# Local attention of a tuned transformer stack: V as weights, turned probabilities moving, denominators by products with ones

## The chip, the core and the metric

The kernel runs on one core of one Trainium2 chip. The metric is the device time of one execution in microseconds (us); lower is better. TensorE multiplies matrices into PSUM, VectorE and ScalarE read PSUM and do the elementwise work, GpSimd helps on SBUF, SyncE issues transfers. All arrays of this case fit in SBUF, and the program is written out by hand: each engine has its own list of instructions, and semaphores order them against each other.

## What is computed

A chain of four layers on x of shape (8, 128, 128): a cross attention with relative positions, a quantised feed-forward layer, a second cross attention, and the stage that this document is about, a local-attention transformer of depth 2. It takes the 8 blocks of x one by one, 128 tokens each; the window is 64.

```python
DIM, DEPTH, HEADS, DIM_HEAD, WINDOW = 128, 2, 8, 64, 64

def local_attention(q, k, v):            # q, k, v: (b, 8 heads, n, 64)
    ...                                  # windows of 64 look at themselves and at the one before
    sim = jnp.einsum('bhwid,bhwjd->bhwij', bq, bk)
    sim = jnp.where(mask, -jnp.finfo(sim.dtype).max, sim)
    attn = jax.nn.softmax(sim, axis=-1)
    out = jnp.einsum('bhwij,bhwjd->bhwid', attn, bv)
    ...

def _layer(x, wqkv, qs, ksc, wo, lg, lb, w1, b1, w2, b2):
    h = shift_token(x)
    q, k, v = jnp.split(h @ wqkv, 3, axis=-1)          # then split into heads
    q, k = rotary_xpos(l2norm(q) * qs, l2norm(k) * ksc)
    o = local_attention(q, k, v)
    x = x + o.transpose(0, 2, 1, 3).reshape(b, n, 512) @ wo
    ...                                  # shift, layer norm, w1, a * gelu(g), w2, residual
```

## The kernel before

The stages run one after another; the first three take about the first 320 us and are not touched. In the local stage a *tile* is one block n of 128 tokens in layer l, with all 8 heads; there are 8 tiles in each of 2 layers. Everything is float32, and a float32 product shows as two pairs of weight load and matmul in the trace, a turn (a transpose through TensorE) as one. A tile goes through these steps; the names are those of the functions.

- `qkv` (TensorE): three products of 512 columns into banks 0 to 2. ScalarE squares q and k (`square`) and copies V to `VL` (`take_v`).
- `rotate` (VectorE): rotary tables and sums of squares; `head_root` (ScalarE) and `unit_norm` (VectorE) finish the norm of the heads.
- `turn_qk` (TensorE, 8 turns into banks 5 and 6), `take_turned_qk` (ScalarE, two copies).
- `score` (TensorE): the band mask and 8 heads of 64 rows, even and odd heads in the two halves of the rows, into banks 3 and 4. `largest` (VectorE) takes the row maximum, `shift` (TensorE) subtracts it, `exponential` (ScalarE) writes the probabilities, tokens on the partitions.
- `turn_p` (TensorE, 8 turns into banks 5 and 6), `take_turned_p` (ScalarE, two copies to `P1`: keys on the partitions).
- `weigh` (TensorE, L547): for each head the turned probabilities are the weights and V of that head moves, with a 65th column of ones, so that the same product gives the denominator. The output has tokens on the partitions.
- `divide_output` (VectorE): a reciprocal of the 8 denominators of each token (L1002) and a multiply into `LO` (L1006).
- `turn_o` (TensorE, L521, 4 turns of the output into bank 7), `take_turned_o` (ScalarE, L1215, one copy to `LOT`), `project_o` (TensorE, L527, 4 products with `wo`), `add_output` (VectorE, L996).

TensorE's order in the loop over tiles n sets how the steps interleave: `shift(n)`, `qkv(n+2)`, `turn_qk(n+1)`, `turn_o(n-1)`, `turn_p(n)`, `project_o(n-1)`, `score(n+1)`, `weigh(n)`. VectorE's is `largest(n)`, `divide_output(n-1)`, `unit_norm(n+1)`, `rotate(n+2)`, `add_output(n-1)`. ScalarE's is `exponential(n)`, `square(n+2)`, `take_turned_qk(n+1)`, `take_turned_o(n-1)`, `take_v(n+2)`, `take_turned_p(n)`, `head_root(n+2)`. In tiles 6 and 7 parts of the feed-forward layer come in between (`turn_norm`, `hidden`, `gate`), and after tile 7 follow `hidden(2)`, `turn_o(7)`, `project_o(7)` and `down(0)`, while ScalarE loads an activation table between its last `take_gelu` and `take_turned_o(7)`.

Of the kernel before, what the change touches and what calls it, by code (L numbers as in the profile page):

```python
# [17 lines left out]
ALU = mybir.AluOpType  # L18
ACT = mybir.ActivationFunctionType
AX = mybir.AxisListType  # L20

P = 128
# [62 lines left out]
def build(nc, x_d, ctxT_d, maskT_d, const_d, l0_d, ffn0_d, l1_d, f_d, out_d):  # L85
    with ExitStack() as stack:
# [108 lines left out]
        VL = view(blkf, 9216, 3, LH, LD + 1)  # L195
        LO = view(blkf, 10776, 2, 512)
        LOT = full[:, 0, 0:512].rearrange("p (a b) -> p a b", a=4)
# [30 lines left out]
        def _(pe):  # L228
# [285 lines left out]
            def turn_o(l, n):  # L514
                pe.wait_ge(sem("lo_norm"), NB * l + n + 1)
                if n >= 1:
                    pe.wait_ge(sem("z"), NB + 10 * l + n)
                else:
                    pe.wait_ge(sem("zT"), 2 * l + 2)
                for j in range(4):  # L520
                    i = tr(ps[:, 7, P * j:P * (j + 1)], LO[:, n % 2, P * j:P * (j + 1)], ident)  # L521
                i.then_inc(sem("loT_ps"), 1)

            def project_o(l, n):
                pe.wait_ge(sem("loT"), NB * l + n + 1)
                for j in range(4):
                    i = mm(ps[:, 7, 0:P], LOT[:, j, :], w_f[:, l, F_WO + P * j:F_WO + P * (j + 1)], start=(j == 0), stop=(j == 3))  # L527
                i.then_inc(sem("lwo_ps"), 1)
# [11 lines left out]
            def weigh(l, n):  # L540
                b = NB * l
                pe.wait_ge(sem("qkv_read"), b + n + 1)
                for h in range(LH):
                    if h % 4 == 0:
                        pe.wait_ge(sem("p_turned"), 2 * (b + n) + h // 4 + 1)
                    s = 2 * (h % 4) + h // 4
                    i = mm(ps[:, 5 + h // 4, 65 * (h % 4):65 * (h % 4 + 1)], P1[:, n % 2, P * h:P * (h + 1)],  # L547
                           VL[:, n % 3, s, :], start=(h % 4 == 0), stop=True, skip_group_check=True)
                i.then_inc(sem("lo_ps"), 1)
# [54 lines left out]
            for l in range(2):  # L604
                for n in range(NB):
# [7 lines left out]
                    if n >= 1:  # L613
                        turn_o(l, n - 1)
                    turn_p(l, n)
                    if n >= 1:
                        project_o(l, n - 1)
# [10 lines left out]
                turn_o(l, NB - 1)  # L628
# [20 lines left out]
        def _(dve):  # L649
# [348 lines left out]
            def divide_output(l, n):  # L998
                b = NB * l
                dve.wait_ge(sem("lo_ps"), b + n + 1)  # L1000
                o = ps[:, 5:7, 0:260].rearrange("p b (h d) -> p b h d", h=4)
                step(v.reciprocal(lrec[:, :].rearrange("p (b h) -> p b h", b=2), o[:, :, :, LD]))  # L1002
                settle()
                if n >= 2:
                    dve.wait_ge(sem("loT_ps"), b + n - 1)
                v.tensor_tensor(LO[:, n % 2, :].rearrange("p (h b d) -> p b h d", b=2, h=4), o[:, :, :, 0:LD],  # L1006
                                lrec[:, :].rearrange("p (b h o) -> p b h o", b=2, h=4).to_broadcast([P, 2, 4, LD]),
                                ALU.mult).then_inc(sem("lo_norm"), 1)
# [60 lines left out]
        def _(act):  # L1069
# [140 lines left out]
            def take_turned_o(l, n):  # L1210
                b = NB * l
                act.wait_ge(sem("loT_ps"), b + n + 1)
                if b + n >= 1:
                    act.wait_ge(sem("lwo_ps"), b + n)
                a(LOT, ps[:, 7, :].rearrange("p (j t) -> p j t", j=4), ACT.Copy).then_inc(sem("loT"), 1)  # L1215

# [53 lines left out]
            for l in range(2):  # L1270
                for n in range(NB):
# [12 lines left out]
                    if n >= 1:  # L1284
                        take_turned_o(l, n - 1)
# [10 lines left out]
                take_turned_o(l, NB - 1)  # L1296
# [22 lines left out]
        def _(pool):  # L1319
# [27 lines left out]
            g_.memset(VL[:, :, :, LD:LD + 1], 1.0).then_inc(sem("pool_zeroed"), 1)  # L1347
            pool.wait_ge(sem("blocks"), 4)
            pool.wait_ge(sem("pool_zeroed"), 1)
# [48 lines left out]
```

## Time and profile before

| | us |
|---|---|
| median of 3 runs (lowest to highest) | 597.12 (596.97 to 600.94) |
| the profiled execution | 598.13 |
| its span | 596.2 |
| TensorE matmul busy in the span | 460.5 (77%) |
| VectorE busy | 416.3 (70%) |
| ScalarE busy | 217.5 (36%) |
| mean granted clock of TensorE | 0.868 of 2.4 GHz |

Engines in the rows: PE is TensorE's matmul, PEld its weight load, DVE is VectorE, ACT is ScalarE, POOL is GpSimd. L527 is line 527 of the kernel. A row in order of time reads: start, length, engine, line, operation, out<-in, shapes, count, and in brackets how long the engine had been idle and what ended that. Rows of the same kind that follow each other are merged into one, so its length spans them all. Matmuls are pipelined: each shows some 0.2 to 0.3 us of its own length while they start 0.05 to 0.2 us apart. The granted clock (PEclk) is 1.00 at 2.4 GHz and 0.50 at 1.2 GHz.

### The profile page before, as it was taken

Reading aid. Unit: us, or ns where it says so; the run is one execution under the profiler, and the core shown is the slowest. Engines: PE = TensorE matmul, PEld = TensorE weight load, DVE = VectorE, ACT = ScalarE, POOL = GpSimd, SP = SyncE. Lnnn points to the kernel's source line nnn. Section 1 sums busy time; section 2 is a strip of 40 time slices with the busy share of each in tenths; the row PEclk is TensorE's granted clock in tenths of the full one; section 3 lists DMA queues with packets and bytes.
Section 4 is the critical chain, followed back from the end, with each engine's and each line's share of the span. In section 5 each row is a group of like instructions: output and inputs, shape, how many; then the busy total and the mean of one; then the engine's idle time right before and its main releaser. Section 6 shows DMA issues by size and latency. Waiting matters only on the chain.

```text
span 596.2 us, 10352 instructions
## 1 busy us (share of the span) xinstructions
PE 460.5 (77%) x4308; PEld 350.0 (59%) x4309; DVE 416.3 (70%) x834; ACT 217.5 (36%) x365; POOL 28.2 (5%) x21
## 2 busy tenths in 40 slices
PE   4379999989824377889886568989787588987946
PEld 2268999979611235767784136667563456766733
DVE  6989977892287888988624638788526668878331
ACT  2324333331233123334432234454534445454431
POOL 3400000000000040000000000000000000001010
PEclk9879999997655577878976869999989899997998
DMA  8200000001000000000000000000000000000000
GB/s 346 106 2 2 3 4 3 3 2 36 1 1 0 0 1 1 1 0 2 1 0 2 0 0 1 1 1 1 1 1 0 0 1 2 1 1 1 1 18 18
DMA packets 1630, 8.43 MB, mean 14 GB/s; under 512 B 177, under 2 KB 177, under 8 KB 1329
## 3 DMA queue, kind: packets, MB, share of 16 engines
q1 hardware_dynamic: 1584, 7.78, 3.4%
q8 instruction: 34, 0.56, 0.4%
q14 instruction: 12, 0.09, 0.0%
HBM read 7.26 MB, written 0.52 MB: 13 GB/s over the span
## 4 chain that ended last, share of the span: by engine, by line
PE 54%; DVE 31%; ACT 8%; issue 6%; DMA 1%; ACTq 0%; DVEq 0%
PE ps L232 15%; PE ps L477 8%; PE ps L329 5%; PE ps L547 4%; PE ps L583 3%; PE ps L449 3%; DVE blk L730 3%; PE ps L527 3%; PE ps L537 2%; DVE m L923 2%; DVE PT L927 2%; PE ps L307 2%; DVE blk L744 2%; PE ps L592 2%; PE ps L244 1%
## 5 line engine op out<-in xcount | busy, mean ns | idle before, releaser
L477 PE MATMUL ps<-w_f,full 128*128 128x512 f32 x96 | 49.3, 654 | 5.4 <-DVE blk L969 3.7
L232 PE MATMUL ps<-blk,stA 128*128 128x64 bf16 (+1 forms) x576 | 47.5, 223 | 3.5 <-issue 3.5
L1128 ACT ACTIVATE St<-ps 128x512 f32<-128x512 f32 x32 | 19.2, 599 | 73.3 <-PE ps L232 73.3
L965 DVE TENSOR_TENSOR blk<-ps,tabs 128x1024 f32<-128x1024 f32 x16 | 19.6, 1224 | 35.5 <-ACT blk L1198 35.5
L232 PEld LDWEIGHTS ps<-blk,stA 128*128 128x128 bf16 x576 | 33.6, 102 | 13.4 <-issue 6.8
L329 PE MATMUL ps<-V,PT 128*64 128x9 f32 x512 | 38.5, 214 | 0.0
L329 PEld LDWEIGHTS ps<-V,PT 128*64 128x64 f32 x512 | 36.3, 155 | 2.5
L449 PEld LDWEIGHTS ps<-V,PT 128*128 128x128 f32 x256 | 37.7, 234 | 0.0
L232 PE MATMUL ps<-blk,stB 128*128 128x64 bf16 (+1 forms) x288 | 37.7, 222 | 0.0
L1173 ACT ACTIVATE PT<-PT 128x1024 f32<-128x1024 f32 x16 | 16.9, 1057 | 56.8 <-DVE PT L927 56.8
L449 PE MATMUL ps<-V,PT 128*128 128x9 f32 x256 | 37.1, 283 | 0.0
L477 PEld LDWEIGHTS ps<-w_f,full 128*128 128x128 f32 x96 | 20.0, 212 | 27.8 <-issue 24.6
L547 PE MATMUL ps<-blk,PT 128*128 128x65 f32 x256 | 31.6, 276 | 0.0
L547 PEld LDWEIGHTS ps<-blk,PT 128*128 128x128 f32 x256 | 30.0, 192 | 2.4 <-issue 1.0
L841 DVE TENSOR_REDUCE mneg<-ps 128x4 bf16<-128x512 f32 x32 | 21.9, 687 | 12.9 <-PE ps L307 12.8
L730 DVE TENSOR_TENSOR blk<-blk,const 128x512 bf16<-128x512 bf16 x48 | 30.1, 682 | 0.0
L730 DVE TENSOR_TENSOR blk<-part,const 128x512 bf16<-128x512 bf16 x48 | 30.0, 682 | 0.0
L436 PE MATMUL ps<-const,PT 128*128 128x128 f32 x128 | 20.3, 311 | 12.5 <-ACT PT L1180 10.9
L232 PEld LDWEIGHTS ps<-blk,stB 128*128 128x128 bf16 x288 | 26.6, 100 | 5.3 <-issue 2.7
L923 DVE TENSOR_REDUCE m<-ps 128x8 f32<-128x1024 f32 x16 | 19.5, 1221 | 13.3 <-PE ps L232 13.3
L436 PEld LDWEIGHTS ps<-const,PT 128*128 128x128 f32 x128 | 17.2, 162 | 18.6 <-ACT PT L1173 16.3
L537 PE MATMUL ps<-const,PT 128*128 128x128 f32 x128 | 17.8, 285 | 12.6 <-ACT blk L1223 12.6
(200 smaller groups left out, 1021.7 us busy)
## 6 DMA issues: line engine op xcount, KB each, us to landing
w_f<-f_dram SPq DMA_DIRECT2D x2, 1689.0 KB, 13.7
w_x<-l_dram SPq DMA_DIRECT2D x1, 774.0 KB, 6.6
w_f<-ffn_dram SPq DMA_DIRECT2D x1, 561.0 KB, 8.3
w_f<-l_dram SPq DMA_DIRECT2D x1, 514.0 KB, 3.6
X<-x_dram SPq DMA_DIRECT2D x1, 512.0 KB, 3.6
ctxT<-ctxT_dram SPq DMA_DIRECT2D x1, 512.0 KB, 4.8
OT<-maskT_dram SPq DMA_DIRECT2D x1, 512.0 KB, 7.4
out_dram<-Z SPq DMA_DIRECT2D x2, 256.0 KB, 2.0
```

The source lines that it names most:

```text
L232: return mm(out, l, r, start=start, stop=False, skip_group_check=True)
L329: i = mm(o[:, n % 4, h, :], pt[:, h, n, q:q + 64], V[:, n, HG * g + h, :], start=(n % 4 == 0 and h == 0), stop=True, skip_group_check=True)
L436: i = tr(ps[:, 4 + c, P * j:P * (j + 1)], S1[:, u % 2, P * (4 * c + j):P * (4 * c + j + 1)], ident)
L449: i = mm(o[:, n % 4, h, :], P1[:, u % 2, P * h:P * (h + 1)], V[:, n, HG * g + h, :], start=(n % 4 == 0 and h == 0), stop=True, skip_group_ ...
L477: i = mm(ps[:, c, :], hT[:, n, :], W[:, F_QKV + 512 * c:F_QKV + 512 * (c + 1)], start=True, stop=True)
L537: i = tr(ps[:, 5 + c, P * j:P * (j + 1)], S1[:, n % 2, P * (4 * c + j):P * (4 * c + j + 1)], ident)
L547: i = mm(ps[:, 5 + h // 4, 65 * (h % 4):65 * (h % 4 + 1)], P1[:, n % 2, P * h:P * (h + 1)], VL[:, n % 3, s, :], start=(h % 4 == 0), stop=T ...
L730: i = v.tensor_tensor(ring[:, c % RING, b, :, :, :], src.to_broadcast([P, NB, QC, HG]), keep.to_broadcast([P, NB, QC, HG]), ALU.mult)
L841: v.tensor_reduce(mneg[:, c % 2, :], ps[:, 4 + c % 2, :].rearrange("p (j k) -> p j k", j=4), AX.X, ALU.max).then_inc(sem("chunk_max"), 1)
L923: step(v.tensor_reduce(m1[:, u % 2, :], s, AX.X, ALU.max))
L965: step(v.tensor_tensor(heads(R[:, n % 2, :]), u, tab[:, 0].to_broadcast([P, 2, LH, LD]), ALU.mult))
L1128: a(St[:, i % 2, :], ps[:, i % 4, :], ACT.Copy).then_inc(sem("st_copied"), 1)
```

## The change

`weigh` swaps its operands. V of a head becomes the weights (64 columns) and the turned probabilities move (128 columns), so the output has the head's 64 features on half of the partitions and the tokens along the free axis: it is already turned. Even heads write partitions 0 to 63, odd heads 64 to 127, of bank 5. The denominators come from 8 more products with a matrix of ones as weights, into bank 6, where each of 64 partitions holds the same sums. `divide_output` takes the reciprocal of all of bank 6 (128 x 512) into the new buffer `over`, and multiplies bank 5 by it straight into `LOT`, which becomes double. `turn_o` and `take_turned_o` go; `project_o` stands where `turn_o` stood. `VL` loses its column of ones. `weigh` waits for both halves of `P1` at its start.

```diff
--- before.py
+++ after.py
@@ -192,9 +192,9 @@
         T2 = view(blkf, 5120, T)
         QT = view(blkf, 6144, 2, 4, P)
         KT = view(blkf, 7168, 2, 4, P)
-        VL = view(blkf, 9216, 3, LH, LD + 1)
-        LO = view(blkf, 10776, 2, 512)
-        LOT = full[:, 0, 0:512].rearrange("p (a b) -> p a b", a=4)
+        VL = view(blkf, 9216, 3, LH, LD)
+        over = view(blkf, 10776, 512)
+        LOT = full[:, 0, :].rearrange("p (s a b) -> p s a b", s=2, a=4)
         hT = full[:, 1, :].rearrange("p (n t) -> p n t", n=NB)
 
         ps = stack.enter_context(nc.psum_tensor("ps", [P, 8, 512], F32))
@@ -511,20 +511,15 @@
                             lneg[:, n % 2, 4 * c:4 * c + 4].rearrange("p (h o) -> p h o", o=1).to_broadcast([P, 4, P]))
                 i.then_inc(sem("lshifted"), 1)
 
-            def turn_o(l, n):
+            def project_o(l, n):
                 pe.wait_ge(sem("lo_norm"), NB * l + n + 1)
                 if n >= 1:
                     pe.wait_ge(sem("z"), NB + 10 * l + n)
                 else:
                     pe.wait_ge(sem("zT"), 2 * l + 2)
                 for j in range(4):
-                    i = tr(ps[:, 7, P * j:P * (j + 1)], LO[:, n % 2, P * j:P * (j + 1)], ident)
-                i.then_inc(sem("loT_ps"), 1)
-
-            def project_o(l, n):
-                pe.wait_ge(sem("loT"), NB * l + n + 1)
-                for j in range(4):
-                    i = mm(ps[:, 7, 0:P], LOT[:, j, :], w_f[:, l, F_WO + P * j:F_WO + P * (j + 1)], start=(j == 0), stop=(j == 3))
+                    i = mm(ps[:, 7, 0:P], LOT[:, n % 2, j, :], w_f[:, l, F_WO + P * j:F_WO + P * (j + 1)],
+                           start=(j == 0), stop=(j == 3))
                 i.then_inc(sem("lwo_ps"), 1)
 
             def turn_p(l, n):
@@ -540,12 +535,17 @@
             def weigh(l, n):
                 b = NB * l
                 pe.wait_ge(sem("qkv_read"), b + n + 1)
+                pe.wait_ge(sem("p_turned"), 2 * (b + n) + 2)
                 for h in range(LH):
-                    if h % 4 == 0:
-                        pe.wait_ge(sem("p_turned"), 2 * (b + n) + h // 4 + 1)
-                    s = 2 * (h % 4) + h // 4
-                    i = mm(ps[:, 5 + h // 4, 65 * (h % 4):65 * (h % 4 + 1)], P1[:, n % 2, P * h:P * (h + 1)],
-                           VL[:, n % 3, s, :], start=(h % 4 == 0), stop=True, skip_group_check=True)
+                    d, j = LD * (h % 2), h // 2
+                    mm(ps[d:d + LD, 5, P * j:P * (j + 1)], VL[:, n % 3, h, :],
+                       P1[:, n % 2, P * (4 * (h % 2) + j):P * (4 * (h % 2) + j + 1)],
+                       start=(j == 0), stop=True, skip_group_check=True)
+                for h in range(LH):
+                    d, j = LD * (h % 2), h // 2
+                    i = mm(ps[d:d + LD, 6, P * j:P * (j + 1)], ones[:, 0:LD],
+                           P1[:, n % 2, P * (4 * (h % 2) + j):P * (4 * (h % 2) + j + 1)],
+                           start=(j == 0), stop=True, skip_group_check=True)
                 i.then_inc(sem("lo_ps"), 1)
 
 
@@ -611,10 +611,8 @@
                     if n + 1 < NB:
                         turn_qk(l, n + 1)
                     if n >= 1:
-                        turn_o(l, n - 1)
+                        project_o(l, n - 1)
                     turn_p(l, n)
-                    if n >= 1:
-                        project_o(l, n - 1)
                     if n + 1 < NB:
                         score(l, n + 1)
                     if n == 6:
@@ -625,7 +623,6 @@
                     if n == 5:
                         shift_tokens(l, 0)
                 hidden(l, 2)
-                turn_o(l, NB - 1)
                 project_o(l, NB - 1)
                 down(l, 0)
                 shift_tokens(l, 1)
@@ -998,14 +995,12 @@
             def divide_output(l, n):
                 b = NB * l
                 dve.wait_ge(sem("lo_ps"), b + n + 1)
-                o = ps[:, 5:7, 0:260].rearrange("p b (h d) -> p b h d", h=4)
-                step(v.reciprocal(lrec[:, :].rearrange("p (b h) -> p b h", b=2), o[:, :, :, LD]))
-                settle()
-                if n >= 2:
-                    dve.wait_ge(sem("loT_ps"), b + n - 1)
-                v.tensor_tensor(LO[:, n % 2, :].rearrange("p (h b d) -> p b h d", b=2, h=4), o[:, :, :, 0:LD],
-                                lrec[:, :].rearrange("p (b h o) -> p b h o", b=2, h=4).to_broadcast([P, 2, 4, LD]),
-                                ALU.mult).then_inc(sem("lo_norm"), 1)
+                step(v.reciprocal(over, ps[:, 6, :]))
+                settle()
+                if b + n >= 2:
+                    dve.wait_ge(sem("lwo_ps"), b + n - 1)
+                v.tensor_tensor(LOT[:, n % 2, :, :].rearrange("p a b -> p (a b)"), ps[:, 5, :], over, ALU.mult)\
+                    .then_inc(sem("lo_norm"), 1)
 
             unit_banks = ((0, 1), (3, 4), (0, 1), (3, 4), (5, 6), (3, 4))
 
@@ -1207,13 +1202,6 @@
                 act.wait_ge(sem("ss"), NB * l + n + 1)
                 root(ss[:, :], lss[:, :], lr0[:, :], "root")
 
-            def take_turned_o(l, n):
-                b = NB * l
-                act.wait_ge(sem("loT_ps"), b + n + 1)
-                if b + n >= 1:
-                    act.wait_ge(sem("lwo_ps"), b + n)
-                a(LOT, ps[:, 7, :].rearrange("p (j t) -> p j t", j=4), ACT.Copy).then_inc(sem("loT"), 1)
-
             def take_turned_qk(l, n):
                 b = NB * l
                 act.wait_ge(sem("qkT_ps"), b + n + 1)
@@ -1281,8 +1269,6 @@
                         take_turned_qk(l, n + 1)
                     if n == 6:
                         norm_root(4 + 2 * l)
-                    if n >= 1:
-                        take_turned_o(l, n - 1)
                     if n + 2 < NB:
                         take_v(l, n + 2)
                     take_turned_p(l, n)
@@ -1293,7 +1279,6 @@
                 take_gelu(l, 1)
                 take_gelu(l, 2)
                 nc.scalar.preload_act_table_set(roots)
-                take_turned_o(l, NB - 1)
                 take_halves(l, 1)
                 if l == 0:
                     take_turned_z(1, 0)
@@ -1344,9 +1329,8 @@
             add_bias(1, w_x1, 3 * NB)
 
             pool.wait_ge(sem("scores1"), G * NB)
-            g_.memset(VL[:, :, :, LD:LD + 1], 1.0).then_inc(sem("pool_zeroed"), 1)
             pool.wait_ge(sem("blocks"), 4)
-            pool.wait_ge(sem("pool_zeroed"), 1)
+            pool.wait_ge(sem("bias_added"), 2)
             g_.memset(hT[64:128, :, 0:1], 0.0).then_inc(sem("local_zeroed"), 1)
             bias_row = lambda t: t.rearrange("p (o e) -> p o e", o=1).to_broadcast([P, 4, P])
             for l in range(2):
```

TensorE's list in a full tile of layer 0, from the shift on. The names are the functions above: L232 with `lneg` is `shift`, L477 `qkv`, L491 `turn_qk`, L521 `turn_o`, L537 `turn_p`, L527 `project_o`, L232 with `band_b` and `blk` `score`, L547 `weigh`. Before:

```order
L232 MATMUL ps<-lneg,ident_b 128x512 x2
L477 MATMUL ps<-w_f,full 128x512 x3
L491 MATMUL ps<-const,blk 128x128 x8
L521 MATMUL ps<-const,blk 128x128 x4
L537 MATMUL ps<-const,PT 128x128 x8
L527 MATMUL ps<-w_f,full 128x128 x4
L232 MATMUL ps<-band_b,ident_b 128x512 x2
L232 MATMUL ps<-blk 128x128 x8
L547 MATMUL ps<-blk,PT 128x65 x8
```

The same tile in the changed kernel, where L521 is `project_o`, L532 `turn_p`, L541 and L546 the two halves of `weigh`:

```order
L232 MATMUL ps<-lneg,ident_b 128x512 x2
L477 MATMUL ps<-w_f,full 128x512 x3
L491 MATMUL ps<-const,blk 128x128 x8
L521 MATMUL ps<-w_f,full 128x128 x4
L532 MATMUL ps<-const,PT 128x128 x8
L232 MATMUL ps<-band_b,ident_b 128x512 x2
L232 MATMUL ps<-blk 128x128 x8
L541 MATMUL ps<-PT,blk 64x128 x8
L546 MATMUL ps<-PT,ones 64x128 x8
```

The four turns are gone, the projection stands ahead of `turn_p`, and `weigh` has 16 products instead of 8.

VectorE's list in the same place, from the row maximum to the first step of `rotate`. Before:

```order
L991 TENSOR_REDUCE lneg<-ps 128x8
L1002 RECIPROCAL lrec<-ps 128x8
L1006 TENSOR_TENSOR blk<-ps,lrec 128x2x4x64
L680 TENSOR_TENSOR lnt<-lr 128x16
L682 SCALAR_TENSOR_TENSOR lnt<-lnt,ss 128x16
L684 SCALAR_TENSOR_TENSOR lr<-lnt,lr 128x16
L983 TENSOR_TENSOR blk<-blk,lr 128x1024
L965 TENSOR_TENSOR blk<-ps,tabs 128x1024
```

In the changed kernel (`over` lies in the buffer `blk`, `LOT` in `full`):

```order
L988 TENSOR_REDUCE lneg<-ps 128x8
L998 RECIPROCAL blk<-ps 128x512
L1002 TENSOR_TENSOR full<-ps,blk 128x512
L677 TENSOR_TENSOR lnt<-lr 128x16
L679 SCALAR_TENSOR_TENSOR lnt<-lnt,ss 128x16
L681 SCALAR_TENSOR_TENSOR lr<-lnt,lr 128x16
L980 TENSOR_TENSOR blk<-blk,lr 128x1024
L962 TENSOR_TENSOR blk<-ps,tabs 128x1024
```

The order of the list is the same; the reciprocal has grown from 8 to 512 elements in each partition.

TensorE's list at a layer's end, from the last unit of the hidden layer's first half (L583, weights 85 wide) to `down` (L592). Before:

```order
L583 MATMUL ps<-YT,w_f 85x512 x2
L521 MATMUL ps<-const,blk 128x128 x4
L527 MATMUL ps<-w_f,full 128x128 x4
L592 MATMUL ps<-w_f,PT 128x128 x12
L559 MATMUL ps<-Z,const 128x256
```

And in the changed kernel:

```order
L583 MATMUL ps<-YT,w_f 85x512 x2
L521 MATMUL ps<-w_f,full 128x128 x4
L592 MATMUL ps<-w_f,PT 128x128 x12
L559 MATMUL ps<-Z,const 128x256
```

Here the turns go and the projection follows the hidden unit at once.

## Rows read from the trace of the kernel before

**Rows 1.** The page, part 4: the chain that ended last, share of the span by engine
```profile
PE 54%; DVE 31%; ACT 8%; issue 6%; DMA 1%; ACTq 0%; DVEq 0%
```

**Rows 2.** Order of time, one full tile of layer 0: start us, us, engine, line, op [idle before]
```profile
405.35 0.61 PE L232 MATMUL ps<-lneg,ident_b 128*128 128x512 bf16 x2
405.41 0.21 DVE L1002 RECIPROCAL lrec<-ps 128x8 f32<-128x8 f32 x1
...
405.65 0.69 DVE L1006 TENSOR_TENSOR blk<-ps,lrec 128x512 f32<-128x512 f32 x1
405.79 2.74 PE L477 MATMUL ps<-w_f,full 128*128 128x512 f32 x6
...
406.26 0.16 DVE L680 TENSOR_TENSOR lnt<-lr 128x16 f32<-128x16 f32 x1
...
406.88 1.22 DVE L983 TENSOR_TENSOR blk<-blk,lr 128x1024 f32<-128x1024 f32 x1
...
408.37 1.04 PE L491 MATMUL ps<-const,blk 128*128 128x128 f32 x8
408.57 1.03 ACT L1198 ACTIVATE blk<-ps 128x1024 f32<-128x1024 f32 x1 [1.55 <-PE ps L477]
...
409.24 0.60 PE L521 MATMUL ps<-const,blk 128*128 128x128 f32 x4
...
409.63 1.22 DVE L965 TENSOR_TENSOR blk<-ps,tabs 128x1024 f32<-128x1024 f32 x1 [1.52 <-ACT blk L1198]
...
410.71 1.06 PE L537 MATMUL ps<-const,PT 128*128 128x128 f32 x8 [0.87 <-ACT blk L1223]
...
411.61 1.06 PE L527 MATMUL ps<-w_f,full 128*128 128x128 f32 x8
...
412.51 0.59 PE L232 MATMUL ps<-band_b,ident_b 128*128 128x512 bf16 x2
...
413.03 1.16 PE L232 MATMUL ps<-blk 64*128 64x128 f32 x16
...
414.12 2.00 PE L547 MATMUL ps<-blk,PT 128*128 128x65 f32 x16
...
414.82 1.21 DVE L991 TENSOR_REDUCE lneg<-ps 128x8 bf16<-128x1024 f32 x1
...
416.16 0.21 DVE L1002 RECIPROCAL lrec<-ps 128x8 f32<-128x8 f32 x1
```

**Rows 3.** VectorE's groups by form, whole span: xcount | busy us, mean ns | idle before
```profile
L1002 DVE RECIPROCAL lrec<-ps 128x8 f32<-128x8 f32 x16 | 3.3, 206 | 3.9 <-PE ps L547 2.7
...
L767 DVE RECIPROCAL rec<-ps 128x32 f32<-128x32 f32 x8 | 2.8, 352 | 22.6 <-PE ps L329 13.0 <-PE ps L449 9.5
...
L808 DVE RECIPROCAL winv<-wsc 128x1 f32<-128x1 f32 x5 | 0.8, 163 | 0.2
```

**Rows 4.** Order of time, the first attention stage, 64-wide weights, 16 instructions
```profile
99.34 1.10 PE L329 MATMUL ps<-V,PT 128*64 128x9 f32 x16
```

**Rows 5.** Order of time, tiles 6 and 7 of layer 0: reciprocals and a hidden unit
```profile
428.18 0.21 DVE L1002 RECIPROCAL lrec<-ps 128x8 f32<-128x8 f32 x1 [1.09 <-PE ps L547]
...
428.41 1.88 PE L583 MATMUL ps<-YT,w_f 128*128 128x512 f32 x4
...
436.82 0.21 DVE L1002 RECIPROCAL lrec<-ps 128x8 f32<-128x8 f32 x1 [0.26 <-PE ps L547]
```

**Rows 6.** Order of time, end of layer 0: the last output projection
```profile
441.20 1.16 PE L527 MATMUL ps<-w_f,full 128*128 128x128 f32 x8 [2.25 <-ACT full L1215]
```

**Rows 7.** Order of time, TensorE after its two longest holes in the tiles
```profile
419.98 1.09 PE L491 MATMUL ps<-const,blk 128*128 128x128 f32 x8 [2.94 <-DVE blk L983]
...
546.45 1.97 PE L491 MATMUL ps<-const,blk 128*128 128x128 f32 x8 [3.71 <-DVE blk L983]
```

**Rows 8.** Stretches of 10 us: us, busy of each engine, PEclk, DMA share, GB/s
```profile
415.00:425.00 10.00, 6.23 (x51) 4.95 (x51) 7.89 (x24) 4.86 (x11) 1.26 (x1) 1.00 0.01 2
...
545.00:555.00 10.00, 8.14 (x55) 7.21 (x56) 5.47 (x19) 3.34 (x8) 0.31 (x1) 0.67 0.00 0
```

## The prediction

> **What bounds the kernel now.** I read four views, in this order: the page, the order of time through one tile of the local attention, the groups of VectorE by form, and the last tiles of a layer. The page says that TensorE holds 54% of the chain that ended last and VectorE 31% [rows 1], an average over stages. The change touches only the last 240 us of the span, the sixteen tiles (two layers of eight) of local attention, so I read one tile there [rows 2].
>
> A tile takes 10.75 us (reciprocal at 405.41 to reciprocal at 416.16) [rows 2], and most of the sixteen look like it. Two loops run through it, nearly equal. TensorE: the shift at 405.35, three projections, turning q and k (408.37), turning the output (409.24), a wait of 0.87 us for ScalarE's copies of q and k, turning the probabilities (410.71), the output projection (411.61), the next scores (412.51 and 413.03) and `weigh` (414.12 to 416.12) [rows 2]. VectorE: it idles 1.52 us for ScalarE's square, begins `rotate` at 409.63 and works on without a gap to the end of the row maximum, 414.82 + 1.21 = 416.03. From the shift to there is 10.68 us: the next shift waits for that maximum. So faster matmuls alone save almost nothing in a full tile, since the maximum still ends at 10.68.
>
> A third loop is not critical today: the reciprocal (405.41), the multiply (405.65), Newton step (406.26), head norm (406.88 to 408.10), then turning q and k (408.37) [rows 2]. TensorE is busy with the projections until then (405.79 + 2.74 = 408.53), so VectorE's path hides behind them with next to no slack. This is the path on which the change puts work.
>
> **Part by part, in one full tile.**
>
> *Removed.* Four turns of the output, 409.24 to the next free slot (0.47 us of TensorE), and one copy by ScalarE. The turns fill a hole: after them TensorE waits 0.87 us anyway [rows 2]. The projection (8 instructions, 411.61 to 412.51, 0.90 us) moves into their place, into the same hole, ahead of `turn_p`. So the stretch from `turn_p` to the reciprocal loses 0.90 us.
>
> *Weigh.* Before: 16 instructions (8 products, two passes each), 2.00 us, 0.12 us apart [rows 2]. After: 32 instructions, V or ones as 64-wide weights, 128 columns moving, heads alternating between the halves of the output. The trace has no such instruction. Two neighbours bound it. The scores alternate between the two halves of the rows with 128 columns moving: 16 instructions in 1.16 us, of which about 0.29 is one's own length, so (1.16 - 0.29)/15 = 0.058 us apart [rows 2]. Instructions with 64-wide weights and 9 columns, in one half: (1.10 - 0.20)/15 = 0.060 [rows 4], so the weight loads can keep that pace. Full-width products with 128 columns: (1.06 - 0.27)/7 = 0.113 [rows 2]. If the column halves overlap as the row halves do, `weigh` takes 31 x 0.058 + 0.25 = 2.05 us; if not, 31 x 0.11 + 0.25 = 3.65 us. I take 2.05 because the scores are nearest in pattern, and keep 3.65.
>
> *Reciprocal.* Before, 8 elements per partition; after, 512. This decides the case. The trace has reciprocals of 1, 8 and 32 elements at 163, 206 and 352 ns [rows 3]. From 8 to 32 they rise by 146/24 = 6.1 ns an element, against about 1 ns for ordinary VectorE work: 1220 ns for 1024 elements, 690 for 512 [rows 2]. Extended, 206 + 504 x 6.1 = 3.28 us, against 0.21. The lower bound is that long reciprocals stream like the multiply, 0.69 us; the rise could then come from the strided read that both of these have, which the new one hasn't. I take 3.28: two sizes on one line that also passes near 163 at one element speak for a cost of each element.
>
> *The new loop.* Put the reciprocal's start at 0. The multiply starts at 3.3, the Newton step 0.61 later (406.26 - 405.65), the head norm 0.62 after it, ending 1.22 later: 5.75. Turning q and k, 0.27 behind (408.10 to 408.37): 6.02. To `turn_p`, which includes ScalarE's copies, 2.34 (410.71 - 408.37): 8.36; the projection fits in front. To the scores 0.90: 9.26. Scores 1.61 (412.51 to 414.12): 10.87. `weigh` 2.05, to the next reciprocal: 12.92 us. Each duration not named otherwise is from [rows 2]. Do the others fit under it? VectorE works 5.75 + 5.19 (409.63 to 414.82) + 1.21 = 12.15 us of it, so it still has 0.8 us over. The new period is 12.92 against 10.75: +2.17. TensorE's wait before turning q and k grows from nothing to 6.02 - 3.2 = 2.8 us (the projections still end 3.2 after the shift).
>
> *Per layer.* Reciprocals 1 to 5: five periods. I give the first 0.2 less, since the tile that opens a layer is not yet in the rhythm: 1.95 + 4 x 2.17 = +10.6. Tile 6 took 12.02 (416.16 to 428.18); the same sum plus 0.45 for four turns of the norm (4 x 0.113) gives 13.4, or 14.5 if VectorE is held up by about 1.1 there as it was before; +1.9 in the middle. Tile 7 took 8.64 (428.18 to 436.82) [rows 5]: now the projection waits for the multiply, 4.0 us after the reciprocal's start, then 0.9 + 0.9 for `turn_p`, 1.72 for one unit of the hidden layer [rows 5] and 2.05 for `weigh`: 9.6, +0.9. At the layer's end the projection began 441.20 - 436.82 = 4.38 us after the reciprocal, held by an activation-table load and the copy on ScalarE [rows 5, 6]. Now nothing but the multiply holds it, 3.3 + 0.69 + 0.05 = 4.04: -0.3. The gain that the removed copy could bring here is eaten by the reciprocal. A layer: 10.6 + 1.9 + 0.9 - 0.3 = +13.1; both, +26.2.
>
> *The clock.* A tile now has a 2.8 us hole on TensorE. In this trace it idled 2.94 us before 419.98 and stayed at 2.4 GHz (granted 1.00), and idled 3.71 before 546.45 and fell to 1.2 GHz, granted 0.67 over that stretch [rows 7, 8]. There the same eight turns took 1.97 us for 1.09, about 0.9 more [rows 7]. The new hole lies just below the harmless one, but there are a dozen. `turn_p`, scores or `weigh` at half speed cost 1 to 2 us each time. I put in four such falls, +6; none to ten is possible, 0 to +18.
>
> *The sum.* The profiled execution took 598.1 us (span 596.2), the median of the runs is 597.1; I add to the median. 597.1 + 26.2 + 6 = 629 us. The memset of the ones column that goes, and the new wait of GpSimd in its place, lie far from any bound: nothing.
>
> **Rivals.**
> - *A, the forecast, 0.50:* reciprocal about 3.3 us, halves overlap. 629, itself 618 to 643.
> - *B, the column halves run one after the other, 0.27:* `weigh` 3.65, period 14.5, +1.6 in the 14 tiles where `weigh` lies in the loop, +22: 651. For it: nothing in the trace shows column halves side by side. Against it: row halves do it. The Trainium skill is of two minds: "TensorEngine Tiling (Array Packing)", Key Properties, lets different tiles load and multiply in parallel; "TensorE: Matmul & The Clock Gate", Part 3, The mechanism, says that a weight load overlaps running matmuls only when its row group differs, which speaks against this change.
> - *C, a long reciprocal streams, 0.10:* 0.69 us. The third loop falls to 12.92 - 2.59 = 10.3, below the 10.7 of the row maximum, so full tiles stand still. The ends gain: in tile 7 the projection no longer waits for ScalarE (-1.2), and at the layer's end down-projection can start some 2.2 earlier. -3.4 a layer: 590, faster by 1.1%. It decides once the reciprocal takes under 3.3 - 2.1 = 1.2 us. Against it: 352 ns for 32 elements.
> - *D, a longer step for each element, 0.13:* eight of VectorE's steps of 1.04 ns (1220 - 690 ns over 512 elements [rows 2]) are 8.3 ns, 4.4 us for 512, +1.1 in 14 tiles and a longer hole, some +17: 646. Against it: 6.1 measured. The Trainium skill, "VectorE: DVE Perf Modes", the 8-slice walkthrough, "First, the fixed hardware budget", says that the reciprocal repeats its divide steps eight times; the rise in [rows 3] agrees in kind and is a little smaller.
>
> **The numbers.** Slower by over 1% (about what a measurement here can tell from no change): A, B and D, 0.90, less the chance that clock and gaps favour it: 0.89. Faster by over 1%: the better part of C, 0.06. Within 1%: 0.05. The range leaves out C (0.10) and B with D together or A with many falls of the clock: 612 to 662.
>
> **What would show it.** The reciprocal's row: 16 instructions of 128x512, 3.3 us each. Reciprocals 12.9 us apart in full tiles. A wait of turning q and k for the head norm, near 2.8 us. `weigh` with its 32 instructions 0.058 apart (A) or 0.11 (B). No wait for the copy at the layer's end. Wrong would be a reciprocal under 1.2 us, or a period of 12.1 or less, which would mean that VectorE alone bounds the tile.

## The result and the profile after

| | before | changed |
|---|---|---|
| median, us | 599.03 | 632.43 |
| runs, us | 596.97 to 608.08 (4) | 630.03 to 636.68 (4) |
| span of the profiled execution, us | 596.2 | 628.3 |
| mean granted clock | 0.868 | 0.845 |

The changed kernel is slower by 5.8%: ratio 1.0577, 95% interval 1.0479 to 1.0676. The forecast was 629 us. The execution of 608.08 us fell in a slower state of the chip and is left out of the ratio, though not of the median.

The page of the changed kernel, the shares of the chain that ended last and the costliest group:

```profile
PE 49%; DVE 41%; ACT 4%; issue 4%; DMA 1%; DVEq 0%; ACTq 0%
...
L998 DVE RECIPROCAL blk<-ps 128x512 f32<-128x512 f32 x16 | 53.7, 3356 | 10.1 <-PE ps L546 10.1
```

VectorE's share of the chain rose from 31% [rows 1] to 41%, and the reciprocal is the costliest group of the kernel: 16 instructions of 3.36 us, 53.7 us, where the old one took 0.21 us each [rows 3].

One full tile of layer 0 in order of time, the same stretch of work as in [rows 2] (start, length, engine, line, operation, idle before):

```profile
400.63 0.61 PE L232 MATMUL ps<-lneg,ident_b 128*128 128x512 bf16 x2
400.75 3.36 DVE L998 RECIPROCAL blk<-ps 128x512 f32<-128x512 f32 x1 [0.67 <-PE ps L546]
...
401.08 2.74 PE L477 MATMUL ps<-w_f,full 128*128 128x512 f32 x6
...
404.14 0.69 DVE L1002 TENSOR_TENSOR full<-ps,blk 128x512 f32<-128x512 f32 x1
...
405.36 1.23 DVE L980 TENSOR_TENSOR blk<-blk,lr 128x1024 f32<-128x1024 f32 x1
...
406.64 1.97 PE L491 MATMUL ps<-const,blk 128*128 128x128 f32 x8 [2.83 <-DVE blk L980]
...
408.41 1.67 PE L521 MATMUL ps<-w_f,full 128*128 128x128 f32 x8
...
411.31 1.16 PE L232 MATMUL ps<-blk 64*128 64x128 f32 x16
...
412.40 1.09 PE L541 MATMUL ps<-PT,blk 128*64 128x128 f32 x16
412.52 1.22 DVE L988 TENSOR_REDUCE lneg<-ps 128x8 bf16<-128x1024 f32 x1 [0.75 <-PE ps L232]
...
413.33 1.04 PE L546 MATMUL ps<-PT,ones 128*64 128x128 f32 x16
...
414.42 3.36 DVE L998 RECIPROCAL blk<-ps 128x512 f32<-128x512 f32 x1 [0.68 <-PE ps L546]
```

From reciprocal to reciprocal the tile takes 13.67 us, against 10.75 [rows 2]. The row maximum (L988) is done at 413.74, before the reciprocal, and holds nothing. The reciprocal runs from 400.75 to 404.11, the multiply and the head norm (L980) follow to 406.59, and only then can TensorE turn q and k (L491): it waited 2.83 us. The eight turns behind it ran slowly: L491 took 1.97 us, where it took 1.04 before. Two stretches of 10 us show why (busy time of each engine, then the granted clock):

```profile
400.00:410.00 10.00, 7.17 (x39) 5.07 (x36) 9.09 (x11) 3.40 (x5) 0.00 (x0) 0.83 0.00 0
410.00:420.00 10.00, 7.49 (x67) 4.82 (x65) 8.41 (x11) 3.77 (x7) 0.00 (x0) 1.00 0.00 0
```

In the first, with the wait in it, the clock was at 1.2 GHz for a part (granted 0.83 as a mean); in the second it was at 2.4 GHz throughout (1.00). The same 1.97 us stands in nine of the ten full tiles, all but the first of layer 0, and in both tiles 6, where the wait before the turns was 4.88 us. The first full tile of layer 0, the one without a fall, took 12.78 us.

The end of layer 0, tile 7, as in [rows 5, 6]:

```profile
442.35 3.36 DVE L998 RECIPROCAL blk<-ps 128x512 f32<-128x512 f32 x1 [1.26 <-PE ps L546]
...
446.49 1.44 PE L521 MATMUL ps<-w_f,full 128*128 128x128 f32 x8 [1.93 <-DVE full L1002]
...
447.73 1.91 PE L532 MATMUL ps<-const,PT 128*128 128x128 f32 x8
...
449.43 2.48 PE L583 MATMUL ps<-YT,w_f 128*128 128x512 f32 x4
...
453.86 3.36 DVE L998 RECIPROCAL blk<-ps 128x512 f32<-128x512 f32 x1 [0.43 <-PE ps L546]
...
458.00 1.16 PE L521 MATMUL ps<-w_f,full 128*128 128x128 f32 x8 [2.31 <-DVE full L1002]
```

Tile 7 took 453.86 - 442.35 = 11.51 us against 8.64; the last projection started 4.14 us after the reciprocal, against 4.38.

### The profile page after: what moved, and what is told of

It reads as the page before. It is cut to its first block, busy times and chain, and to the rows that moved or that the text cites. A ratio compares the mean times of both kernels' runs of the same rounds, so it can differ in the third digit from the quotient of the medians.

```text
span 628.3 us, 10706 instructions
## 1 busy us (share of the span) xinstructions
PE 471.4 (75%) x4500; PEld 356.9 (57%) x4501; DVE 463.4 (74%) x834; ACT 211.5 (34%) x349; POOL 27.7 (4%) x20
## 4 chain that ended last, share of the span: by engine, by line
PE 49%; DVE 41%; ACT 4%; issue 4%; DMA 1%; DVEq 0%; ACTq 0%
PE ps L232 13%; DVE blk L998 9%; PE ps L329 5%; DVE blk L727 4%; PE ps L491 4%; PE ps L449 4%; PE ps L521 3%; PE ps L583 3%; DVE blk L980 3%; PE ps L477 2%; PE ps L541 2%; PE ps L532 2%; PE ps L546 2%; DVE full L1002 2%; DVE PT L924 2%
## 5 line engine op out<-in xcount | busy, mean ns | idle before, releaser
L998 DVE RECIPROCAL blk<-ps 128x512 f32<-128x512 f32 x16 | 53.7, 3356 | 10.1 <-PE ps L546 10.1
L491 PE MATMUL ps<-const,blk 128*128 128x128 f32 x128 | 27.9, 390 | 39.6 <-DVE blk L980 39.6
L232 PE MATMUL ps<-blk,stA 128*128 128x64 bf16 (+1 forms) x576 | 49.8, 227 | 4.3 <-issue 4.3
L491 PEld LDWEIGHTS ps<-const,blk 128*128 128x128 f32 x128 | 22.4, 203 | 50.9 <-DVE blk L980 49.7
L477 PE MATMUL ps<-w_f,full 128*128 128x512 f32 x96 | 46.3, 620 | 5.4 <-DVE blk L966 3.7
L232 PEld LDWEIGHTS ps<-blk,stA 128*128 128x128 bf16 x576 | 34.8, 104 | 15.0 <-issue 9.1
L232 PE MATMUL ps<-blk,stB 128*128 128x64 bf16 (+1 forms) x288 | 39.6, 228 | 0.0
L477 PEld LDWEIGHTS ps<-w_f,full 128*128 128x128 f32 x96 | 19.1, 201 | 25.8 <-issue 22.6
L521 PE MATMUL ps<-w_f,full 128*128 128x128 f32 x128 | 24.5, 355 | 8.5 <-DVE full L1002 8.5
L232 PEld LDWEIGHTS ps<-blk,stB 128*128 128x128 bf16 x288 | 27.4, 103 | 5.7 <-issue 3.3
L521 PEld LDWEIGHTS ps<-w_f,full 128*128 128x128 f32 x128 | 23.6, 276 | 11.9 <-DVE full L1002 11.9
```

The source lines that it names most:

```text
L232: return mm(out, l, r, start=start, stop=False, skip_group_check=True)
L477: i = mm(ps[:, c, :], hT[:, n, :], W[:, F_QKV + 512 * c:F_QKV + 512 * (c + 1)], start=True, stop=True)
L491: i = tr(ps[:, 5 + c, P * j:P * (j + 1)], R[:, n % 2, P * (4 * c + j):P * (4 * c + j + 1)], ident)
L521: i = mm(ps[:, 7, 0:P], LOT[:, n % 2, j, :], w_f[:, l, F_WO + P * j:F_WO + P * (j + 1)], start=(j == 0), stop=(j == 3))
L998: step(v.reciprocal(over, ps[:, 6, :]))
```

## The experiments

All ratios below are to runs of the kernel before on the same chip, with 95% intervals. Where an expectation speaks of the fourth experiment, it means the one with the reciprocal on ScalarE.

### Reciprocals of 8 and of 256 elements

In the first kernel the reciprocal of the changed kernel is cut from 512 elements to 8, in the second to 256; the multiply still covers 512 and reads the few reciprocals again and again, so neither kernel divides rightly. What is left out is only VectorE's work on the other elements.

```diff
-step(v.reciprocal(over, ps[:, 6, :]))
+step(v.reciprocal(over[:, 0:8], ps[:, 6, 0:8]))        # second kernel: 0:256
-v.tensor_tensor(LOT..., ps[:, 5, :], over, ALU.mult)
+v.tensor_tensor(LOT..., ps[:, 5, :], over[:, 0:8] repeated 64 times, ALU.mult)
```

> The changed kernel with one thing less: the reciprocal covers 8 of the 512 elements of a partition, and the multiply reads those 8 over and over (the division is wrong, everything else is done). Theory (the long reciprocal is the whole loss): the reciprocal takes 0.21 us, full tiles fall back to 10.7 us, held by the row maximum as before, and the time is 590 us, faster than before, since the ends of the layers gain from the copy that is gone. Rival (the 16 products of weigh, the halves of the columns or the new order of the projection cost time as well): full tiles stay above 10.8 us and the time above 597.

> The changed kernel with a reciprocal over 256 of the 512 elements, used twice (the division is wrong). Theory (a cost of 6.2 ns for each element): the reciprocal takes 0.21 + 248 x 6.2 ns = 1.75 us, 1.6 less than now; the tile falls by 1.6 and by what the clock gives back, to 11.3 us, and the time to about 600 us. Rival (a cost of the large form as such, whatever its length): the reciprocal stays above 3 us and the time at 630.

Measured: 591.4 us with 8 elements (ratio 0.990, 0.985 to 0.995; expected 590) and 600.4 us with 256 (1.0043, 1.0003 to 1.0083; expected about 600). The reciprocals of each kernel, first the kernel with 8 elements, its group and a full tile:

```profile
L998 DVE RECIPROCAL blk<-ps 128x8 f32<-128x8 f32 x16 | 3.2, 201 | 3.4 <-PE ps L546 3.4
```

```profile
384.47 0.20 DVE L998 RECIPROCAL blk<-ps 128x8 f32<-128x8 f32 x1
...
384.61 0.61 PE L232 MATMUL ps<-lneg,ident_b 128*128 128x512 bf16 x2 [0.90 <-DVE lneg L988]
...
395.22 0.20 DVE L998 RECIPROCAL blk<-ps 128x8 f32<-128x8 f32 x1
```

And with 256 elements:

```profile
L998 DVE RECIPROCAL blk<-ps 128x256 f32<-128x256 f32 x16 | 28.1, 1756 | 9.0 <-PE ps L546 9.0
```

```profile
395.35 1.76 DVE L998 RECIPROCAL blk<-ps 128x256 f32<-128x256 f32 x1 [0.61 <-PE ps L546]
...
406.54 1.76 DVE L998 RECIPROCAL blk<-ps 128x256 f32<-128x256 f32 x1 [0.62 <-PE ps L546]
```

With 8 elements the tile is back at 10.75 us and TensorE waits 0.90 us for the row maximum (L988) before its shift: everything else that the change does costs nothing in a full tile, and the ends of the layers gain (tile 7 takes 7.64 us against 8.64). The lengths lie on a line: 201 ns for 8 elements, 352 for 32, 1756 for 256, 3356 for 512. From 8 to 512 that is 3155/504 = 6.26 ns an element. The middle kernel excludes a fixed cost of a large form. Its tile of 11.19 us is 1.59 shorter than the changed kernel's 12.78 at full clock, for a reciprocal 1.60 shorter: from there on the third loop sets the pace, us for us.

### The kernel before with the long reciprocal added

```diff
 step(v.reciprocal(lrec..., o[:, :, :, LD]))
+step(v.reciprocal(rest[:, 0:512], ps[:, 5, :]))
 settle()
```

> The kernel before with one thing more: beside its reciprocal of 8 elements VectorE takes one of 128x512 from PSUM in divide_output, whose result nobody reads. Theory (the long reciprocal sits in the loop through turning q and k): the tile becomes 14.1 us at full clock (3.4 + 0.2 in place of 0.2, and the output projection still between turn_p and the scores), 14.8 if the clock falls in the hole, and the time is 640 to 650 us. Rival (VectorE has 1.5 us to spare in a tile, so only the excess counts): tile 10.75 + 3.4 - 1.5 = 12.6 us, 620 us or less.

Measured: 644.3 us, ratio 1.0792 (1.0747 to 1.0837), inside the 640 to 650 expected. The added reciprocal and the turning of q and k in a full tile:

```profile
402.57 3.31 DVE L1003 RECIPROCAL rest<-ps 128x512 f32<-128x512 f32 x1
...
408.42 1.09 PE L491 MATMUL ps<-const,blk 128*128 128x128 f32 x8 [3.00 <-DVE blk L983]
...
416.35 3.31 DVE L1003 RECIPROCAL rest<-ps 128x512 f32<-128x512 f32 x1
```

The tile is 13.78 us, 0.3 shorter than expected, and 3.0 longer than before for 3.3 us more of VectorE: nearly the whole instruction lies on the loop, though VectorE had 1.5 us to spare in a tile. The rival, which counted only the excess over that, falls. Against this kernel the changed one, without turns and copy, is faster by 2% of the time before (1.0577 against 1.0792), some 12 us, although its clock fell in the full tiles and this one's did not.

The clock in this kernel stood at 2.4 GHz through the full tiles, though TensorE's wait is 3.00 us and longer than the 2.83 of the changed kernel:

```profile
370.00:420.00 50.00, 37.70 (x265) 27.12 (x263) 43.32 (x53) 20.06 (x37) 0.00 (x0) 1.00 0.00 1
```

The turns took 1.09 us in all ten full tiles. So the length of the wait alone does not decide whether the clock falls.

### The hole filled with idle products

```diff
 qkv(l, n + 2)
+if n >= 1:
+    pe.wait_ge(sem("zT"), 2 * l + 2)
+    for _ in range(20):
+        mm(ps[:, 7, 256:512], ident_b, band_b twice, start=True, stop=True)
```

> The changed kernel with 20 idle products (128x256, bf16, into an unused part of bank 7, 2.2 us in all at 2.4 GHz) behind the projections of q, k and v in tiles 1 to 5 of a layer, where TensorE otherwise waits 2.8 us for the head norm. Nothing reads them. Theory (the hole is what lets the clock fall to 1.2 GHz in each full tile, and the half clock costs 0.75 us of 13.67): the granted clock stays at 1.00 through those tiles, their period falls to 12.9 us and the time to 623 us. Rival (the clock falls for another reason, or half clock costs nothing on the loop): no change, 630, or slower, if the added products delay the turns.

Measured: 626.8 us, ratio 1.0483 (1.0381 to 1.0585), 4 us above the 623 expected. TensorE's list around the filled hole and VectorE's reciprocals, then the clock:

```profile
401.40 2.35 PE L614 MATMUL ps<-band_b,ident_b 128*128 128x256 bf16 x20
404.39 1.09 PE L491 MATMUL ps<-const,blk 128*128 128x128 f32 x8 [0.65 <-DVE blk L986]
```

```profile
398.50 3.36 DVE L1004 RECIPROCAL blk<-ps 128x512 f32<-128x512 f32 x1 [0.63 <-PE ps L546]
...
411.28 3.36 DVE L1004 RECIPROCAL blk<-ps 128x512 f32<-128x512 f32 x1 [0.63 <-PE ps L546]
```

```profile
370.00:420.00 50.00, 45.93 (x403) 34.18 (x403) 46.39 (x56) 19.62 (x35) 0.00 (x0) 1.00 0.00 1
```

The clock stayed at 2.4 GHz in the full tiles, the turns took 1.09 us in all ten full tiles, and the tile fell from 13.67 to 12.78 us: half clock cost 0.89 us in each, 8 us for the nine. The profiled executions differ by only 2.9 us of span, since this one lost 3.9 between the layers, where its clock was lower (53.21 us from the last reciprocal of layer 0 to the first of layer 1, against 49.31). The interval overlaps that of the changed kernel, so what is shown is the gain of the tiles and not one of the whole time.

### The order of the heads in weigh

```diff
-for h in range(LH):
+for h in (0, 2, 4, 6, 1, 3, 5, 7):       # both loops of weigh
```

> The changed kernel with the heads of weigh in another order: first the four even heads (outputs on partitions 0 to 63), then the four odd ones (64 to 127), for V and for the ones; the work is the same. Theory (two matmuls run side by side only when neighbours lie in different column halves): the instructions come 0.107 us apart instead of 0.057, weigh takes 3.5 us instead of 2.0, the tile grows by 1.5 and the time to about 650 us. Rival (64 wide weights are enough, whatever the order): 0.057 apart, 630 us.

Measured: 637.6 us, ratio 1.0623 (1.0528 to 1.0717), where about 650 was expected. The interval overlaps that of the changed kernel, so a loss of the whole time is not shown; the trace shows one in the tile. `weigh` in order of time; L541 are the products with V, L546 those with ones, and the last row is the shift behind it:

```profile
399.90 1.25 PE L541 MATMUL ps<-PT,blk 128*64 128x128 f32 x13
...
400.89 0.32 PE L546 MATMUL ps<-PT,ones 128*64 128x128 f32 x1
400.99 0.27 PE L541 MATMUL ps<-PT,blk 128*64 128x128 f32 x1
...
401.21 0.27 PE L541 MATMUL ps<-PT,blk 128*64 128x128 f32 x1
...
402.40 0.39 PE L232 MATMUL ps<-lneg,ident_b 128*128 128x512 bf16 x1
```

The 32 instructions take 402.40 - 399.90 = 2.50 us, against 1.91 (412.40 to 414.31) with alternating heads, and 3.5 by the first theory. A full tile without a fall of the clock takes 13.38 us against 12.78, the same 0.6 more. The records show what I had not thought of: the first product with ones (an even head, by its place in the list) starts at 400.89, before the last three instructions with V (odd heads), which start from 400.99 to 401.21. TensorE had taken up work for the idle half from further down its list. So neither theory holds. The order matters, but the two halves are filled from a stretch of the list, not from neighbours alone.

The clock fell in only four of the ten full tiles here (14.25 to 14.34 us long, the others 13.37 or 13.38), with a wait of TensorE of 2.82 us in tiles with a fall and in tiles without.

### The reciprocal on ScalarE

```diff
+def invert(l, n):                     # ScalarE, ahead of exponential(n + 1)
+    step(a(over, ps[:, 6, :], ACT.Ln))
+    settle()
+    a(over, over, ACT.Exp, scale=-1.0).then_inc(sem("over"), 1)
 def divide_output(l, n):              # VectorE
-    step(v.reciprocal(over, ps[:, 6, :]))
+    if n == NB - 1: step(v.reciprocal(over, ps[:, 6, :]))
+    else:           dve.wait_ge(sem("over"), (NB - 1) * l + n + 1)
```

> The changed kernel with the reciprocal on ScalarE as exp(-ln x), two passes over 128x512 of 0.6 us, for tiles 0 to 6 of a layer; tile 7 keeps VectorE's, since the table of gelu is loaded then. Theory: the way from weigh to the multiply takes 1.3 us instead of 3.4, so the third loop falls to about 11.0 us, a little over the 10.7 of the row maximum; the layers' ends gain as in the first experiment but for tile 7's own reciprocal: 595 to 598 us, the same as before. Rival (ScalarE becomes late with the exponential and the square behind the two passes): tiles of 12 us or more, 615 us.

Measured: 600.7 us, ratio 1.0042 (1.0010 to 1.0075), 3 us above the range expected. A full tile, then the turning of q and k in tile 6:

```profile
384.33 0.60 ACT L1212 ACTIVATE blk<-ps 128x512 f32<-128x512 f32 x1 [0.23 <-PE ps L546]
384.96 0.63 ACT L1214 ACTIVATE blk<-blk 128x512 f32<-128x512 f32 x1
...
384.98 0.61 PE L232 MATMUL ps<-lneg,ident_b 128*128 128x512 bf16 x2 [0.70 <-DVE lneg L988]
...
385.68 0.69 DVE L1005 TENSOR_TENSOR full<-ps,blk 128x512 f32<-128x512 f32 x1 [0.75 <-issue]
...
396.42 0.69 DVE L1005 TENSOR_TENSOR full<-ps,blk 128x512 f32<-128x512 f32 x1 [0.74 <-issue]
```

```profile
421.44 1.97 PE L491 MATMUL ps<-const,blk 128*128 128x128 f32 x8 [3.61 <-DVE blk L980]
```

From the start of the first pass to the multiply it takes 1.35 us. The multiply (L1005) comes 10.74 us after the one before, and TensorE waits 0.70 us for the row maximum: full tiles are where they were before the change. ScalarE is not late. What is above the expectation lies in the main in tile 6 of layer 0, where TensorE waited 3.61 us, the clock fell, and 14.5 us went by (multiply to multiply, 417.91 to 432.42) against 12.02 before. Tile 7, whose long reciprocal was in the expectation, took 9.83 against 8.64.

### Division before the turn in tile 7, and the hole of tile 6 filled

The first kernel has the reciprocal of tiles 0 to 6 on ScalarE, as in the experiment above, and this in tile 7:

```diff
+def normalise_p(l):                   # VectorE, in tile 7 only, after divide_output(6)
+    step(v.tensor_reduce(lrec, S1 by heads, AX.X, ALU.add)); settle()
+    step(v.reciprocal(lrec, lrec)); settle()
+    v.tensor_tensor(S1, S1, lrec, ALU.mult).then_inc(sem("p_normed"), 1)
 # TensorE, tile 7: hidden(l, 1) ahead of turn_p; no products with ones
 # divide_output(l, 7): a copy of ps[:, 5] to LOT
```

The second kernel adds the following, and the third puts it into the kernel before:

```diff
 shift(l, n)
+if n == 6:
+    for _ in range(24):
+        mm(ps[:, 7, 256:512], ident_b, band_b twice, start=True, stop=True)
```

> The kernel of the fourth experiment, with the last reciprocal over 512 elements gone too: in tile 7 VectorE sums the probabilities of each head (128x1024, 1.2 us), takes the reciprocal of 8 elements and multiplies the probabilities before they are turned (1.2 us); TensorE does its second hidden unit in the meantime, leaves out the products with ones, and the output is only copied. Theory (what holds the layer's end is the 3.4 us reciprocal): the projection of tile 7 comes 3 us earlier in each layer, 594 to 595 us against 597 before. Rival (the turns wait so long for the multiplied probabilities that nothing is won): 600 us, as in the fourth experiment.

> The same with 24 idle products (128x256, bf16, 2.6 us, bank 7) in tile 6 behind the shift, where TensorE waits 3.6 us for VectorE and the clock then falls. Theory (that hole lets the clock fall, as the holes of the changed kernel do, and the half clock costs 1.9 us on the loop): 1.9 us less in each layer, 590 to 591 us. Rival (it costs nothing there): as e7_early_norm.

> The kernel before with the same idle products at the same place. Theory: in the profile of before the clock fell there in layer 1 alone and cost about 1.9 us, so 1 to 2 us less than before, 595 to 596 us; what e8 gains beyond that comes from the swap and the early division. Rival (idle products are only more work): 597 or more.

Measured: 591.9 us (ratio 0.9888, 0.9830 to 0.9946), 590.8 us (0.9866, 0.9815 to 0.9917) and, for the kernel before with the filling, 597.5 us (0.9978, 0.9938 to 1.0017). Expected were 594 to 595, 590 to 591 and 595 to 596; the third, at 597.5, lies where its rival put it. Tile 7 of the first:

```profile
438.32 1.22 DVE L1002 TENSOR_REDUCE lrec<-PT 128x8 f32<-128x1024 f32 x1 [0.16 <-ACT PT L1246]
...
439.58 0.20 DVE L1004 RECIPROCAL lrec<-lrec 128x8 f32<-128x8 f32 x1
...
439.82 1.23 DVE L1006 TENSOR_TENSOR PT<-PT,lrec 128x1024 f32<-128x1024 f32 x1
...
441.19 1.06 PE L534 MATMUL ps<-const,PT 128*128 128x128 f32 x8
...
443.08 1.09 PE L543 MATMUL ps<-PT,blk 128*64 128x128 f32 x16 [0.83 <-ACT PT L1254]
...
444.22 0.69 DVE L1014 COPY full<-ps 128x512 f32<-128x512 f32 x1
```

The three steps of VectorE take 2.7 us for the 3.4 of one reciprocal, and lie beside the second hidden unit (439.21 to 441.09). The filled hole of the second kernel, and the clock over tile 6 without it and with it:

```profile
414.60 2.78 PE L613 MATMUL ps<-band_b,ident_b 128*128 128x256 bf16 x24
...
418.40 1.09 PE L491 MATMUL ps<-const,blk 128*128 128x128 f32 x8 [1.02 <-DVE blk L989]
```

```profile
425.00:435.00 10.00, 8.22 (x62) 7.50 (x64) 6.02 (x21) 3.35 (x7) 0.23 (x1) 0.66 0.00 0
```

```profile
415.00:425.00 10.00, 8.61 (x88) 7.23 (x88) 7.60 (x23) 4.62 (x10) 1.27 (x1) 1.00 0.01 2
```

The turns of q and k take 1.09 us again with the hole filled, where 1.97 stood, and tile 6 of layer 0 takes 12.36 us in place of 14.22. That the second kernel is faster than the first as a whole is not shown, since the intervals overlap; the profiled execution of the first (span 596.3) had the fall, and its other runs may not all have had it. In the kernel before the filling shortened tile 6 of layer 1, the one with a fall, from 14.61 to 12.81 us, but no difference of the whole time can be told, so the filling alone does not earn the 1.1 to 1.3%. They come from the swap with its cheap division and from tile 7's new order together. The first experiment, where the reciprocal takes 0.2 us and the division is not right, came out at 1.0%, with an interval that overlaps both. Tile 7's new order is worth its place with the reciprocal on ScalarE (0.9888 against 1.0042); it was not tried in the kernel before, so how much of the gain needs the swap is not shown. Both kernels are faster than the changed one by far, and than the kernel before by a little over 1%.

## Why the prediction was right

The forecast was 629 us with a range of 612 to 662, slower by over 1% at 0.89, and case A (a reciprocal of 3.3 us, halves that overlap) as the likeliest. By its steps:

- *The reciprocal.* Forecast 3.28 us from two sizes of 8 and 32 elements; measured 3.36. The cost of an element, 6.26 ns, was read off well from [rows 3]. Case C (it streams) and case D (4.4 us) are out. The page of the Trainium skill named beside D, "VectorE: DVE Perf Modes", "First, the fixed hardware budget", states a repeat count of eight; 6.26 ns is six of VectorE's steps of 1.04 ns, so the count does not give the length with that step.
- *Weigh.* Forecast 2.05 us to the next reciprocal; measured 414.42 - 412.40 = 2.02. Case B is out: the column halves overlap as the row halves do. The instructions come (414.31 - 412.40)/32 = 0.060 us apart. The Trainium skill's "TensorEngine Tiling (Array Packing)", Key Properties, agrees with that; the sentence of the Trainium skill's "TensorE: Matmul & The Clock Gate", Part 3, The mechanism, that only another row group lets a weight load overlap, does not, since all these products use all the rows.
- *The loop.* Forecast 12.92 us a full tile at full clock; with the hole filled it was 12.78, so the five full tiles of a layer grew by 10.0 us apart from the clock, for 10.6 in the forecast. The wait before the turns was put at 2.8 and was 2.83. VectorE idled 0.75 us before the row maximum and 0.67 before the reciprocal, so TensorE's part of the loop binds and not VectorE alone, as the sum said.
- *The rest of the change.* Case C's number, 590 us with a short reciprocal, was measured as 591.4. Its parts were a little large: tile 7 gained 1.0 us for the 1.2 forecast, and the stretch from the last reciprocal on gained 1.15 in layer 0 and 1.6 in layer 1 for the 2.2.
- *The clock, the term that was mis-sized.* I put in four falls at 1 to 2 us, +6. It fell in nine of ten full tiles for 0.89 us each, and in tile 7 of each layer: there the projection, the turns and the hidden unit took 1.24 + 1.70 + 2.41 = 5.35 us from start to start, for 3.5 in the forecast. Together about 8 + 3.7 = 11.7, which takes the whole excess in tile 7 as the clock's; where the kernel with the other order of heads had no fall in tile 7 of layer 1, that tile took 10.43 us, against 12.12 in layer 0 with one. The clock also fell in both tiles 6, which no run prices in this kernel.
- *Luck.* What brought the sum back near 629 is that other stretches of this execution ran better than in the profile of before. Between the layers it took 49.3 us from the last reciprocal of layer 0 to the first of layer 1, against 51.1, since `down` ran at full clock (2.84 us, against 4.47); the first reciprocal came 1.65 earlier, though with the reciprocal of 8 elements, and all else of the change in place, it came 0.74 later than before; and tile 6 of layer 1, slow before at 14.61 us, gained 0.4 where the forecast had +1.9, because it took layer 0's 12.02 for both layers. So the path and the prices of the forecast are borne out, and the closeness of the sum is in part chance.

Where the 32.1 us of span went, in us against before:

| | layer 0 | layer 1 | forecast a layer |
|---|---|---|---|
| first to sixth reciprocal | +13.6 | +14.4 | +10.6, clock apart |
| tile 6 | +2.2 | -0.4 | +1.9 |
| tile 7 | +2.9 | +2.9 | +0.9, clock apart |
| before the first, between the layers, after the last | -1.65, -1.8 | -0.05 | -0.3 |

The forecast of -0.3 for the layer's end was met: the last projection of layer 0 starts 0.24 us earlier after its reciprocal. Its reason holds too, since the copy behind the table load is gone and the reciprocal took its place.

Open is what makes the clock fall in a hole of 2.83 us and not in one of 3.00, and why the same hole of 2.82 us, with the other order of heads, had a fall in some tiles and none in others. The runs show only that it does, and that work in the hole prevents it.

## What to carry to other kernels

Count the elements of a partition in each reciprocal before moving a division to another layout: two small reciprocals in the trace give the slope. A denominator that is the same on 64 partitions is 64 times the work per partition, and belongs where it is one number for each row. When an engine has time to spare, ask on which loop the added instruction lies: 3.3 us on VectorE cost 3.0 us a tile with 1.5 us of idle time beside it.

## What the hardware showed that I had not expected

TensorE began matmuls out of the order of its list when their half of the columns was free: a product with ones at 400.89 us, ahead of instructions with V that stand before it in the list and start from 400.99 to 401.21. Two passes of ScalarE, ln and exp over 128x512, lead to the multiply in 1.35 us, where VectorE's reciprocal takes 3.36. And the clock fell in nine of the ten full tiles of the changed kernel, with a wait of 2.83 us on TensorE (2.56 in the first of layer 1, and the same 2.56 in the first of layer 0 without a fall), and in no full tile of the kernel before with the long reciprocal, whose wait was 3.00 us (2.6 in the first of each layer).
